# The softmax shift of a batch as one bias number of the exponential, with the start of the kernel listed anew

## The chip, the cores and the metric

The kernel runs on one core of a Trainium2 chip. The metric is the device time of one execution in microseconds (us); lower is better. TensorE (PE in the tables) multiplies matrices; VectorE (DVE) and ScalarE (ACT) work on tiles of 128 partitions; GpSimd (POOL) takes some elementwise work; SyncE (SP) issues most DMAs.

## The reference, cut to what matters

The input is 4 batches of 1024 tokens with 128 channels. Three layers run one after the other, each with its layer norm and its residual: a feed-forward layer with a router, attention with 16 heads of 8 channels, and the same feed-forward layer again.

```python
x = x + 0.5 * ffn(layernorm(x))        # relu(x @ up.T)**2 @ down.T + two of 8 experts
q, k, v = rotary(layernorm(x) @ qkv_w.T)
attn = einsum('bhqd,bhkd->bhqk', q, k) * SCALE
attn = attn + minimum(pos_k - pos_q, 0) * slopes[h] * 8.0
x = x + (softmax(attn) @ v) @ proj_w.T + proj_b
x = x + 0.5 * ffn(layernorm(x))
```

A softmax may subtract any number from a row's scores before the exponential, since it drops out in the division. The kernel subtracts an upper bound of the scores (a product of the largest norms of q and k), which keeps the exponential in range.

## The kernel before

The tokens are cut into 8 chunks of 512, two for each batch. A job "A" of a chunk is its first feed-forward layer, the second layer norm and q, k and v. A job "C" is the attention's projection and the second feed-forward layer. Attention runs in **quads**: for 4 heads (a group), one chunk of queries and one tile of 128 keys, `score(n)` multiplies keys and queries into the PSUM tile `f_scores` (128 x 2048), `weight(n)` is one exponential on ACT from `f_scores` to `weights`, and `weigh(n)` multiplies these with the values into `f_acc`. There are 256 quads. `f_scores` exists once: `score(n)` waits for the exponential of quad n - 1, and the exponential of quad n waits for `score(n)`. `weights` exists twice. On the diagonal DVE multiplies with a table `ediag` in between.

All engines walk through the same numbered **steps**. The table `PLAN`, together with `FILLS` and `DIAGONALS`, says for each job in which step each of its pieces is issued, on PE (hidden, spread, outs, qk, value, norms, turn, gate), and by fixed offsets on the other engines. Quad n stands in step `HEAD_STEPS + n`; what lies before is called the head here: it holds the A jobs of chunks 0 and 1, which batch 0's attention needs, and the beginning of chunk 2. Each engine works in the order of its list, so a piece that waits holds up all that stands behind it on that engine. In the head, the norm matmul's output and others use `f_acc` and `f_bank_o`; in the rest `f_bank_h` is shared by the pieces of the jobs.

The shift of a batch is made at the end of its second chunk: `norms` (PE) and `largest_norms` (DVE) for q and k, `bound_product` (DVE), `root` (POOL), `bound_minus` (DVE), which leaves -bound for each of 16 heads in `f_minus`. Before the change `fill_shift` (DVE) spreads it over 512 columns (`f_shift`), and `load_shift_rows` copies these rows by DMA into row 4 of each head's 32 rows of the query operand `q_op`; the key operands have 1.0 there, so that the score matmul itself subtracts the bound. `score` waits for these DMAs by `first_loaded` (batch 0) or `qk_loaded`. The other rows of `q_op`, `k_full` and `k_plain` are the parts of q and k, which are stored to DRAM (L780) and loaded again (L821 for batch 0, L2313 later), and rows of positions, which ACT writes (`fill_rows`, L1187).

The exponential of before, and the wait of its quad:

```python
def weight(n):
    act.wait_ge(scores_made, n + 1)
    if n >= 2:
        act.wait_ge(weighed, n - 1)
    nc.scalar.activation(weights[:, n % 2, :, :], scores[:, :, :], ACT.Exp).then_inc(exps_done, 1)
```

Of the kernel before, what the change touches and what calls it, by code (L numbers as in the profile page):

```python
# [21 lines left out]
F32 = mybir.dt.float32  # L22
F32R = mybir.dt.float32r
BF16 = mybir.dt.bfloat16
ALU = mybir.AluOpType
# [428 lines left out]
class Job:  # L454

    def __init__(self, index, kind, chunk, plan):
# [14 lines left out]
        if self.first:  # L471
            self.moments2, self.centre2, self.turn2 = plan["norm2"]
            self.qk, self.value, self.norms = plan["qk"], plan["value"], plan["norms"]
            at["product"] = [step + 1 for step in self.qk]
            at["sums"] = [at["product"][1], at["product"][3]]
            at["high"] = [step + 1 for step in at["sums"]]
            at["square_qk"] = at["high"]
            at["low"] = [step + 1 for step in at["high"]]
            at["largest"] = [step + 1 for step in self.norms]
            at.update(take_xt2=self.turn2 + 1, take_low2=self.turn2 + 1, take_v=self.value[1] + 1,  # L480
                      moments2=self.moments2 + 1, power2=self.moments2 + 1,
                      bound=at["largest"][1] + 1, minus=at["largest"][1] + 2, fill=at["largest"][1] + 2)
            if self.batch >= 1:
                at["fill"] = max(at["fill"], HEAD_STEPS + HALVES * HG * KT * (self.batch - 1) + 6)
# [10 lines left out]
HEAD_STEPS = 222  # L495
FILLS = (2, 69, 151, 118, 6, 109, 51, 59)
DIAGONALS = (136, 133, 156, 137, 141, 142, 144, 123, 132, 125, 146, 122, 139, 147, 131, 128)
PLAN = (
    ("A", 0, dict(front=(0, 0, 0), norm=(-9, -9, -9, 0), route=(8, 13, 18, 23, 28), coef=35, hidden=(3, 7, 12, 21, 25,
        30, 41, 49), spread=(39, 48, 55, 62), outs=(15, 15, 27, 27, 32, 32, 44, 44, 52, 52, 56, 56, 64, 64, 70, 70),  # L500
        residual=77, norm2=(80, 93, 124), qk=(140, 143, 150, 157), value=(152, 152), norms=(168, 183), own=dict(rectify=(10,
        14, 17, 26, 29, 36, 45, 54), square=(11, 20, 24, 31, 34, 42, 47, 58), scale=(46, 50, 57, 65), exp_logits=4,
        take_coef=38, moments2=85, power2=89, take_xt2=127, take_low2=134, take_v=161, product=(145, 153, 162, 166),
        sums=(155, 167), high=(160, 172), low=(164, 175), square_qk=(159, 171), largest=(173, 198), statistics=-9,
        moments=-9, power=-9, take_xt=-9, take_low=-9))),
    ("A", 1, dict(front=(0, 0, 0), norm=(1, 16, 19, 37), route=(43, 53, 60, 67, 72), coef=90, hidden=(61, 68, 73, 78,
        83, 91, 99, 107), spread=(98, 106, 114, 119), outs=(75, 75, 86, 86, 94, 94, 102, 102, 111, 111, 115, 115, 120, 120,
        126, 126), residual=130, norm2=(138, 158, 163), qk=(174, 176, 179, 182), value=(187, 187), norms=(191, 199),
        own=dict(rectify=(63, 71, 76, 84, 87, 96, 103, 112), square=(66, 74, 79, 88, 95, 100, 105, 116), scale=(101, 108,
        117, 121), exp_logits=40, take_coef=92, moments2=148, power2=154, take_xt2=165, take_low2=170, take_v=193,  # L510
        product=(177, 178, 184, 188), sums=(181, 190), high=(186, 196), low=(189, 200), square_qk=(185, 195), largest=(194,
        202), statistics=1, moments=5, power=9, take_xt=22, take_low=33, bound=205, minus=210, fill=212))),
    ("A", 2, dict(front=(0, 0, 0), norm=(97, 113, 129, 222), route=(223, 224, 225, 226, 227), coef=228, hidden=(203,
        208, 214, 221, 227, 230, 231, 232), spread=(230, 231, 232, 233), outs=(223, 223, 224, 224, 225, 225, 226, 226, 233,
        234, 234, 236, 236, 237, 237, 238), residual=239, norm2=(240, 242, 243), qk=(245, 247, 248, 249), value=(250, 251),
        norms=(252, 253), own=dict(xload=77, moments=104, power=110, take_xt=149, take_low=201, rectify=(206, 211, 216, 222,
        228, 231, 232, 233), square=(209, 215, 217, 222, 231, 232, 233, 234)))),
    ("A", 3, dict(front=(0, 0, 0), norm=(222, 227, 233, 235), route=(236, 237, 238, 243, 245), coef=246, hidden=(238,
        239, 240, 241, 242, 255, 256, 257), spread=(248, 255, 256, 257), outs=(245, 246, 247, 249, 250, 251, 252, 253, 254,
        254, 258, 259, 259, 261, 261, 262), residual=263, norm2=(264, 266, 267), qk=(269, 270, 271, 272), value=(273, 274),  # L520
        norms=(275, 276), own=dict(xload=130))),
    ("A", 4, dict(front=(0, 0, 0), norm=(243, 245, 258, 260), route=(261, 262, 263, 264, 265), coef=266, hidden=(262,
        263, 264, 265, 266, 268, 280, 281), spread=(268, 269, 281, 282), outs=(270, 271, 272, 273, 274, 275, 276, 278, 278,
        279, 279, 280, 285, 285, 286, 286), residual=287, norm2=(288, 290, 291), qk=(293, 296, 298, 299), value=(300, 301),
        norms=(303, 304))),
    ("A", 5, dict(front=(0, 0, 0), norm=(266, 268, 282, 284), route=(285, 286, 291, 293, 294), coef=295, hidden=(287,
        288, 289, 290, 292, 302, 307, 308), spread=(297, 303, 307, 308), outs=(293, 294, 294, 295, 296, 297, 297, 298, 300,
        301, 306, 306, 310, 310, 312, 312), residual=313, norm2=(314, 316, 317), qk=(320, 321, 322, 323), value=(324, 325),
        norms=(326, 327))),
    ("A", 6, dict(front=(0, 0, 0), norm=(291, 301, 309, 311), route=(312, 313, 315, 317, 318), coef=319, hidden=(313,  # L530
        314, 315, 316, 318, 329, 330, 331), spread=(321, 329, 330, 331), outs=(319, 320, 322, 323, 324, 325, 326, 327, 328,
        328, 332, 333, 333, 335, 335, 336), residual=337, norm2=(338, 340, 341), qk=(343, 345, 347, 348), value=(349, 350),
        norms=(351, 352))),
    ("C", 0, dict(front=(260, 269, 277), norm=(302, 310, 332, 334), route=(335, 336, 338, 341, 343), coef=344,
        hidden=(336, 337, 338, 339, 340, 353, 354, 355), spread=(346, 353, 354, 355), outs=(343, 344, 345, 346, 346, 347,
        348, 349, 350, 351, 356, 357, 357, 359, 360, 361), residual=362)),
    ("A", 7, dict(front=(0, 0, 0), norm=(316, 334, 356, 358), route=(359, 360, 361, 363, 364), coef=365, hidden=(359,
        360, 361, 362, 368, 369, 370, 371), spread=(369, 370, 371, 372), outs=(363, 363, 364, 364, 365, 366, 366, 368, 373,
        373, 375, 375, 376, 376, 377, 377), residual=378, norm2=(379, 381, 382), qk=(384, 385, 386, 387), value=(388, 389),
        norms=(390, 391))),  # L540
    ("C", 1, dict(front=(292, 302, 305), norm=(336, 357, 372, 374), route=(375, 376, 377, 379, 380), coef=381,
        hidden=(378, 379, 380, 383, 392, 393, 394, 398), spread=(392, 393, 394, 398), outs=(384, 385, 386, 387, 388, 389,
        390, 391, 395, 395, 396, 396, 397, 397, 402, 402), residual=403)),
    ("C", 2, dict(front=(363, 366, 367), norm=(369, 374, 399, 401), route=(402, 403, 404, 405, 406), coef=407,
        hidden=(403, 404, 409, 410, 413, 414, 415, 419), spread=(413, 414, 415, 419), outs=(405, 405, 406, 406, 411, 411,
        412, 412, 416, 416, 417, 417, 418, 418, 423, 423), residual=424)),
    ("C", 3, dict(front=(404, 407, 408), norm=(410, 412, 420, 422), route=(423, 424, 425, 426, 427), coef=428,
        hidden=(424, 425, 430, 431, 434, 435, 436, 440), spread=(434, 435, 436, 440), outs=(426, 426, 427, 427, 432, 432,
        433, 433, 437, 437, 438, 438, 439, 439, 444, 444), residual=445)),
    ("C", 4, dict(front=(425, 428, 429), norm=(432, 434, 441, 443), route=(444, 445, 446, 447, 448), coef=449,  # L550
        hidden=(445, 446, 451, 452, 455, 456, 457, 461), spread=(455, 456, 457, 461), outs=(447, 447, 448, 448, 453, 453,
        454, 454, 458, 458, 459, 459, 460, 460, 465, 465), residual=466)),
    ("C", 5, dict(front=(446, 449, 450), norm=(452, 454, 462, 464), route=(465, 466, 467, 468, 469), coef=470,
        hidden=(466, 467, 472, 473, 476, 477, 478, 479), spread=(476, 477, 478, 479), outs=(468, 468, 469, 469, 474, 474,
# [2084 lines left out]
```

## Time and profile before

| | |
|---|---|
| three runs | 807.15, 807.54, 807.88 us (median 807.54) |
| the profiled execution | 807.31 us, its span 805.5 us |
| PE busy | 742.4 us (92%) |
| ACT busy | 601.2 us (75%) |
| DVE busy | 445.9 us (55%) |
| POOL busy | 211.3 us (26%) |
| granted clock of PE, mean | 0.985 |

The span runs from the first to the last instruction of the profiled execution; 1.8 us of its time lie outside. The first exponential of a quad starts at 83.85 us and the last one at 744.62 us, so there are three stretches: the head, the quads with the jobs' pieces between them, and the rest of the last job. PE's weight loads (PEld) overlap its matmuls, and the ends of matmuls are modelled, so the busy share of PE says less than what it waits for.

### The profile page before, as it was taken

How to read it: one execution, taken by the hardware profiler on the slowest of the kernel's cores; microseconds unless marked ns; L12 is line 12 of the kernel's file. 1: busy time of each engine (PE TensorE's matmuls, PEld its weight loads, DVE VectorE, ACT ScalarE, POOL GpSimd, SP SyncE). 2: the span in 40 equal slices, each digit the busy share in tenths (PEclk: the TensorE clock that was granted, in tenths of full speed). 3: DMA queues.
4: the chain of work that ended last, by engine and by line, in shares of the span. 5: the costliest groups of instructions: out<-in, count | busy, mean ns of one | idle time of the engine just before them, and what ended most of it. 6: DMA issues, size and time to landing. Idle time of an engine off the chain costs nothing.

```text
span 805.5 us, 14520 instructions
## 1 busy us (share of the span) xinstructions
PE 742.4 (92%) x5520; PEld 370.6 (46%) x5520; DVE 445.9 (55%) x1155; ACT 601.2 (75%) x488; POOL 211.3 (26%) x184
## 2 busy tenths in 40 slices
PE   5996989999999999999999999999989999999876
PEld 3883534444444434344354443443434444434664
DVE  5776445826735773655654656445536435354664
ACT  3892578788878878978878888788878878888321
POOL 2125122223412341332332232321121311211443
PEclk9997799999999999999999999999999999999999
DMA  7015323122166120115332200144322002020200
GB/s 244 1 53 165 104 57 83 28 84 71 42 155 162 46 83 4 33 56 151 77 85 67 55 5 18 47 125 107 71 49 57 5 4 60 4 57 5 60 13 18
DMA packets 43966, 52.60 MB, mean 65 GB/s; under 512 B 10154, under 2 KB 28146, under 8 KB 43762
## 3 DMA queue, kind: packets, MB, share of 16 engines
q1 hardware_dynamic: 42066, 50.19, 23.6%
q10 hardware_dynamic: 1824, 1.41, 0.6%
q8 instruction: 46, 0.75, 0.4%
q14 instruction: 30, 0.25, 0.1%
HBM read 31.91 MB, written 19.40 MB: 64 GB/s over the span
## 4 chain that ended last, share of the span: by engine, by line
PE 67%; ACT 18%; DVE 7%; issue 3%; DMA 1%; POOL 0%; POOLq 0%; DVEq 0%; ACTq 0%
PE f_acc L927 22%; ACT weights L1232 17%; PE f_scores L908 14%; PE f_bank_o L1026 14%; PE f_bank_h L882 9%; PE f_bank_c L1005 1%; DVE weights L1572 1%; PE f_scores L882 1%; PE f_bank_h L951 1%; PE f_bank_c L970 1%; ACT f_relu L1160 1%; PE f_acc L1026 1%; PE f_bank_h L1058 1%; PE f_bank_c L972 1%; DVE f_xn L1327 1%
## 5 line engine op out<-in xcount | busy, mean ns | idle before, releaser
L1232 ACT ACTIVATE weights<-f_scores 128x2048 f32<-128x2048 f32 x256 | 480.8, 1878 | 119.7 <-PE f_scores L908 113.4
L927 PE MATMUL f_acc<-weights,v_res 128*9 128x512 f32 x2048 | 269.9, 596 | 8.8 <-DVE weights L1572 7.2
L1026 PEld LDWEIGHTS f_bank_o<-w_out,f_hid 128*128 128x128 f32 x960 | 121.9, 195 | 59.2 <-issue 50.7
L1026 PE MATMUL f_bank_o<-w_out,f_hid 128*128 128x128 f32 x960 | 146.8, 292 | 1.3 <-POOL f_hid L1270 1.0
L1572 DVE TENSOR_TENSOR weights<-weights,ediag 128x512 f32<-128x512 f32 x128 | 92.7, 724 | 97.8 <-ACT weights L1232 97.3
L1270 POOL TENSOR_TENSOR f_hid<-f_hid,f_relu 128x512 f32<-128x512 f32 x56 | 78.9, 1411 | 201.8 <-DVE f_hid L1462 199.4
L1270 POOL TENSOR_TENSOR f_hid<-f_relu 128x512 f32<-128x512 f32 x56 | 60.5, 1083 | 210.7 <-ACT f_relu L1160 210.6
L908 PE MATMUL f_scores<-q_op,k_plain 29*128 29x512 f32 (+3 forms) x768 | 86.6, 440 | 15.2 <-ACT weights L1232 10.3
L908 PEld LDWEIGHTS f_scores<-q_op,k_plain 29*128 29x128 f32 x768 | 37.4, 183 | 131.6 <-ACT weights L1232 110.6
L1160 ACT ACTIVATE f_relu<-f_bank_h 128x512 f32<-128x512 f32 x110 | 65.4, 595 | 31.2 <-PE f_bank_h L882 30.8
L882 PE MATMUL f_bank_h<-xn_t,w_hi 128*128 128x512 f32 x224 | 83.7, 455 | 5.1 <-ACT f_relu L1160 3.2
L1462 DVE TENSOR_TENSOR f_hid<-f_relu,f_bank_c 128x512 f32<-128x512 f32 x56 | 38.4, 685 | 86.3 <-ACT f_relu L1160 62.3
L908 PE MATMUL f_scores<-q_op,k_full 29*128 29x512 f32 (+3 forms) x640 | 62.2, 376 | 6.0 <-ACT weights L1232 5.0
L927 PEld LDWEIGHTS f_acc<-weights,v_res 128*9 128x9 f32 x2048 | 31.7, 88 | 68.3 <-issue 58.4
L882 PEld LDWEIGHTS f_bank_h<-xn_t,w_hi 128*128 128x128 f32 x224 | 35.0, 194 | 52.8 <-issue 27.3
L908 PEld LDWEIGHTS f_scores<-q_op,k_full 29*128 29x128 f32 x640 | 31.7, 186 | 49.1 <-ACT weights L1232 45.4
L882 PE MATMUL f_bank_h<-xn_t,w_lo 128*128 128x512 f32 x112 | 45.6, 407 | 0.0
L1258 POOL TENSOR_TENSOR rstd<-veps,minus_half 128x4 f32<-128x4 f32 x23 | 23.3, 1013 | 70.1 <-DVE veps L450 70.1
L1563 DVE COPY f_o_out<-f_acc 128x512 f32<-128x512 f32 x32 | 22.0, 688 | 30.2 <-PE f_acc L927 30.2
L1286 POOL TENSOR_TENSOR f_squares<-f_roped 128x512 bf16<-128x512 f32 x16 | 19.5, 1216 | 55.8 <-DVE f_roped L1506 42.7
L1005 PE MATMUL f_bank_c<-f_coef_t,spread_rows 128*128 128x512 f32 x58 | 24.0, 414 | 0.8 <-DVE f_hid L1462 0.8
L882 PEld LDWEIGHTS f_bank_h<-xn_t,w_lo 128*128 128x128 f32 x112 | 21.7, 194 | 5.4
(216 smaller groups left out, 716.1 us busy)
## 6 DMA issues: line engine op xcount, KB each, us to landing
q_parts<-f_parts SPq DMA_DIRECT2D x24, 256.0 KB, 3.0
k_parts<-f_parts SPq DMA_DIRECT2D x24, 256.0 KB, 3.0
q_op<-q_parts SPq DMA_DIRECT2D x48, 96.0 KB
k_full<-k_parts SPq DMA_DIRECT2D x48, 96.0 KB
k_plain<-k_parts SPq DMA_DIRECT2D x48, 96.0 KB
o_scratch<-f_o_out SPq DMA_DIRECT2D x128, 18.0 KB
x_ln<-in_L_attn_x_dram SPq DMA_DIRECT2D x8, 256.0 KB, 3.4
rope<-const_rope SPq DMA_DIRECT2D x1, 2048.0 KB, 10.7
```

What stands on the lines that cost most here:

```text
L882: last = nc.tensor.matmul(out, w[:, col:col + P], x_t[:, part, :], start=(i == 0), stop=(i == 2))
L908: last = nc.tensor.matmul(scores[:, j, lo:hi], k_op[rows, g, kt * P:(kt + 1) * P], q_op[rows, g, CHUNK * half + lo:CHUNK * half + hi], sta ...
L927: last = nc.tensor.matmul(acc[BLOCK * j:BLOCK * j + VW, :], v_res[:, c // HALVES, kt, col:col + VW], weights[:, n % 2, j, :], start=(kt == ...
L1005: nc.tensor.matmul(spread_bank(job, m), spread_rows[:, m * P:(m + 1) * P], coef_t[:, :], start=True, stop=True).then_inc(spread, 1)
L1026: last = nc.tensor.matmul(out_bank(job)[:, t * P:(t + 1) * P], hid[:, m, t * P:(t + 1) * P], w_out[:, m, :], start=(m == 0 and t == 0), st ...
L1160: nc.scalar.activation(relu_tile(job, m), hidden_bank(job, m), ACT.Relu).then_inc(relu_ready, 1)
L1232: nc.scalar.activation(weights[:, n % 2, :, :], scores[:, :, :], ACT.Exp).then_inc(exps_done, 1)
L1258: nc.gpsimd.tensor_tensor(rstd[:, which, :], veps[:, which, :], minus_half[:, :], ALU.pow).then_inc(rstd_ready[which], 1)
L1270: nc.gpsimd.tensor_tensor(hid[:, m, :], other, relu_tile(job, m), ALU.mult).then_inc(hid_ready, 1)
L1462: v.tensor_tensor(hid[:, ST + m, :], relu_tile(job, ST + m), spread_bank(job, m), ALU.mult).then_inc(scaled_ready, 1)
L1563: v.tensor_copy(o_out[:, :], acc[:, :]).then_inc(acc_read, 1)
L1572: v.tensor_tensor(at, at, ediag[:, GH * g:GH * (g + 1), :], ALU.mult).then_inc(diag_done, 1)
```

## The change

The shift of a batch becomes one number: the smallest of the 16 heads' -bound, so the largest bound, for all heads. It is given to the exponential as its bias, from the tile `minus_all` (128 partitions x 4 batches). To put the number on all 128 partitions, a matmul (`cast_bounds`, PE) multiplies `f_minus`, broadcast over 128 columns, with the identity: its output holds all 16 values on each partition, and a DVE reduction takes the smallest. The rows `f_shift`, their 32 DMAs and the waits for them are gone; row 4 of `q_op` stays zero, as `fill_rows` writes it. The first exponential of each batch waits for the reduction (`shift_ready`).

```diff
+            def cast_bounds(job):
+                b = job.batch
+                if not job.head:
+                    bank_h_read("cast", job, 0)
+                else:
+                    pe.wait_ge(norms_read, 2 * HEAD_JOBS)
+                pe.wait_ge(bound_step, 4 * b + 3)
+                nc.tensor.matmul(side_bank(job)[:, 0:HEADS], minus[:, b:b + 1].broadcast_to([HEADS, P]),
+                                 ident[0:HEADS, 0:HEADS], start=True, stop=True).then_inc(bounds_cast, 1)
...
             def fill_shift(job):
-                b = job.batch
-                dve.wait_ge(bound_step, 4 * b + 4)
-                for g in range(HG):
...
-                v.tensor_scalar(shift[:, :], rope[0:HEADS, 0, 0:CHUNK], 0.0, minus[:, b:b + 1], ALU.mult,
-                                ALU.add).then_inc(shift_ready, 1)
+                dve.wait_ge(bounds_cast, job.batch + 1)
+                v.tensor_reduce(minus_all[:, job.batch:job.batch + 1], side_bank(job)[:, 0:HEADS], AX.X,
+                                ALU.min).then_inc(shift_ready, 1)
...
-                nc.scalar.activation(weights[:, n % 2, :, :], scores[:, :, :], ACT.Exp).then_inc(exps_done, 1)
+                batch, first = divmod(n, HALVES * HG * KT)
+                if first == 0:
+                    act.wait_ge(shift_ready, batch + 1)
+                nc.scalar.activation(weights[:, n % 2, :, :], scores[:, :, :], ACT.Exp,
+                                     bias=minus_all[:, batch:batch + 1]).then_inc(exps_done, 1)
...
-                    pe.wait_ge(first_loaded[g], 16 * (PART_LOADS + HALVES))
+                    pe.wait_ge(first_loaded[g], 16 * PART_LOADS)
...
-                if step == FIRST_JOB[1].at["fill"] + 1:
-                    sp.wait_ge(shift_ready, 1)
+                if step == FIRST_JOB[1].at["store"][1] + 1:
                     load_half(1, 0, late_plain, late_loaded)
                     load_half(0, 1, first_loaded[1], first_loaded[1])
-                    load_shift_rows(sp, 0, 1, first_loaded[1])
...
-HEAD_STEPS = 222
-FILLS = (2, 69, 151, 118, 6, 109, 51, 59)
+HEAD_STEPS = 223
+FILLS = (78, 58, 177, 118, 125, 134, 128, 122)
```

`PLAN` is a new table as a whole. Counted from the first quad, most pieces of the A jobs of chunks 2 to 6 stand one to a few steps earlier and some of chunk 4's later; those of the C jobs from chunk 3's on stand, but for a few by one step, where they stood. Two places of the new order are shown, as the program's lists have them; the line numbers of the changed kernel are some 8 to 10 off.

PE from chunk 1's q and k to the first quad. `f_xn_t` with `w_hi` and `w_lo` as weights at L882 are the four q and k matmul groups, at L1058 (L1050 after) the values, L1071 (L1063) the norms; `f_bank_h<-xn_t` are hidden tiles of chunk 2, L970 and L972 (L962 and L964) its gate, L908 (L898) `score`. Before, the stretch from the end of the values:

```order
L1058 MATMUL f_scores<-w_lo,f_xn_t 128x128
L1071 MATMUL f_acc<-f_squares,headsum 16x512 x2
L882 MATMUL f_bank_h<-xn_t,w_hi 128x512 x2
L882 MATMUL f_bank_h<-xn_t,w_lo 128x512
L882 MATMUL f_bank_h<-xn_t,w_hi 128x512 x2
...
L908 MATMUL f_scores<-q_op,k_plain 128x128 x4
L908 MATMUL f_scores<-q_op,k_full 128x384 x4
L970 MATMUL f_bank_c<-w_gate,xn_t 128x16
L972 MATMUL f_bank_c<-w_gate,xn_t 128x8
```

The same stretch of the changed kernel, from the last group of chunk 1's k:

```order
L872 MATMUL f_scores<-f_xn_t,w_lo 128x512
L962 MATMUL f_bank_c<-w_gate,xn_t 128x16
...
L1063 MATMUL f_acc<-f_squares,headsum 16x512
L872 MATMUL f_bank_h<-xn_t,w_hi 128x512 x2
L872 MATMUL f_bank_h<-xn_t,w_lo 128x512
L1063 MATMUL f_acc<-f_squares,headsum 16x512
L872 MATMUL f_bank_h<-xn_t,w_hi 128x512 x2
L872 MATMUL f_bank_h<-xn_t,w_lo 128x512
L1074 MATMUL f_acc<-ident,f_minus 128x16
L898 MATMUL f_scores<-q_op,k_plain 128x128 x4
L898 MATMUL f_scores<-q_op,k_full 128x384 x4
L1018 MATMUL f_bank_o<-w_out,f_hid 128x128 x4
```

Before, four hidden tiles stand between the norms and the first score, and the gate behind it. After, the gate and three hidden tiles stand ahead, with the two norm matmuls between the tiles; the values (not in these rows) moved from behind the q and k groups to behind the first of them.

ACT from the transposed second norm of chunk 0 (`f_xn_t<-f_bank_o`) on; `f_parts<-f_roped` is the high part of q or k, `ediag` a table of a head, `q_op` and `k_full` are filled with rows of positions. Before:

```order
L1136 ACTIVATE f_xn_t<-f_bank_o 128x512
L1191 ACTIVATE ediag<-weights,slope 128x128 x12
L1136 ACTIVATE xn_t<-f_bank_h 128x512
L1187 ACTIVATE q_op<-weights,q_add,row_sel 128x1024
L1191 ACTIVATE ediag<-weights,slope 128x128
L1136 ACTIVATE f_parts<-f_roped 128x512
```

and after:

```order
L1141 ACTIVATE f_xn_t<-f_bank_o 128x512
L1192 ACTIVATE q_op<-weights,q_add,row_sel 128x1024
L1192 ACTIVATE k_full<-weights,k_add,row_sel 128x1024 x4
L1196 ACTIVATE ediag<-weights,slope 128x128 x4
L1141 ACTIVATE f_parts<-f_roped 128x512
L1141 ACTIVATE v_res<-f_scores 128x64x8
L1196 ACTIVATE ediag<-weights,slope 128x128 x7
```

Five fills of 1024 columns moved to here from the feed-forward part of the head, and stand ahead of chunk 0's high part of q.

## Rows read from the trace of the kernel before

**Rows 1.** Page: the chain that ended last, by engine.

```profile
PE 67%; ACT 18%; DVE 7%; issue 3%; DMA 1%; POOL 0%; POOLq 0%; DVEq 0%; ACTq 0%
```

**Rows 2.** The chain in order of time: start us, us, what, up to the first quad.

```profile
77.81 4.95 DMA q_op<-f_shift
82.89 0.93 PE f_scores L908 x7
```

**Rows 3.** Timeline of the head's end: start us, us, engine, line, operation [idle before].

```profile
70.14 1.48 DVE L1513 TENSOR_TENSOR f_roped<-f_turn_a,f_turn_b 128x512 f32<-128x512 f32 x1
75.03 0.14 DVE L1544 TENSOR_SCALAR f_minus<-f_bound 16x1 f32<-16x1 f32 x1 [0.65 <-POOL f_bound L1292]
77.12 1.92 SPq L780 DMA_DIRECT2D k_parts<-f_parts  x3
83.49 1.52 SPq L821 DMA_DIRECT2D k_plain<-k_parts  x4
```

**Rows 4.** Windows: busy time by engine, granted clock of PE, DMA share, GB/s.

```profile
76.00:80.00 4.00, 2.74 (x6) 1.16 (x4) 0.52 (x3) 1.13 (x2) 1.68 (x2) 0.50 0.84 261
84.00:88.00 4.00, 3.82 (x23) 3.51 (x24) 2.07 (x12) 3.23 (x3) 0.00 (x0) 0.50 0.48 114
```

**Rows 5.** Exponentials: the group, then the first and the last of 256 in the timeline.

```profile
L1232 ACT ACTIVATE weights<-f_scores 128x2048 f32<-128x2048 f32 x256 | 480.8, 1878 | 119.7 <-PE f_scores L908 113.4
83.85 1.88 ACT L1232 ACTIVATE weights<-f_scores 128x2048 f32<-128x2048 f32 x1 [1.45 <-PE f_scores L908]
744.62 1.88 ACT L1232 ACTIVATE weights<-f_scores 128x2048 f32<-128x2048 f32 x1 [0.17 <-PE f_scores L908]
```

**Rows 6.** Timeline of ACT in one quad, from exponential to exponential.

```profile
98.78 1.88 ACT L1232 ACTIVATE weights<-f_scores 128x2048 f32<-128x2048 f32 x1 [0.64 <-PE f_scores L908]
100.64 0.60 ACT L1160 ACTIVATE f_relu<-f_bank_h 128x512 f32<-128x512 f32 x1
101.27 1.88 ACT L1232 ACTIVATE weights<-f_scores 128x2048 f32<-128x2048 f32 x1
```

**Rows 7.** Groups on ACT by shape: busy us, mean ns of one.

```profile
L309 ACT ACTIVATE proj_t<-prep 128x128 f32<-128x128 f32 x1 | 0.3, 277 | 1.0 <-PE prep L356 1.0
L1136 ACT ACTIVATE xn_t<-f_bank_h 128x512 fp32r<-128x512 f32 x14 | 8.3, 594 | 6.2 <-PE f_bank_h L960 6.2
L1136 ACT ACTIVATE f_parts<-f_roped 128x512 fp32r<-128x512 f32 x4 | 2.5, 631 | 5.3 <-DVE f_roped L1506 4.4 <-DVE f_roped L1513 0.8
L1191 ACT ACTIVATE ediag<-weights,slope 128x128 f32<-128x128 f32 x16 | 5.0, 387 | 0.0
L1187 ACT ACTIVATE k_full<-weights,k_add,row_sel 128x1024 fp32r<-128x1024 f32 x4 | 4.9, 1227 | 0.0
```

**Rows 8.** Timeline of the head from chunk 1's last outputs to chunk 0's loads.

```profile
52.81 1.06 PE L1026 MATMUL f_acc<-w_out,f_hid 128*128 128x128 f32 x8
...
55.25 0.73 PE L882 MATMUL f_bank_o<-f_xn_t,w_hi 128*128 128x512 f32 x2 [0.94 <-DVE f_xn_t L1485]
...
63.71 0.63 ACT L1136 ACTIVATE f_parts<-f_roped 128x512 fp32r<-128x512 f32 x1 [0.61 <-DVE f_roped L1513]
...
66.06 1.81 SPq L780 DMA_DIRECT2D k_parts<-f_parts  x3
...
70.39 1.56 SPq L821 DMA_DIRECT2D k_plain<-k_parts  x4
```

**Rows 9.** Window of the values' line alone (chunk 1): busy PE, PEld.

```profile
69.00:71.00 2.00, 1.55 (x12) 1.41 (x12) 1.00 0.40 138
```

**Rows 10.** The chain in order of time, within the quads.

```profile
614.94 0.51 PE f_scores L908 x4
615.45 1.09 PE f_bank_o L1026 x8
616.54 0.98 PE f_acc L927 x8
```

**Rows 11.** Timeline of POOL: the last batch's root.

```profile
531.04 0.54 POOL L1292 TENSOR_TENSOR f_bound<-f_product,f_half_power 16x1 f32<-16x1 f32 x1 [9.49 <-DVE f_product L1538]
```

More of the change, by code:

```diff
@@ L494 @@
 HEAD_JOBS = 2
[L495 to L497 removed]
+HEAD_STEPS = 223
+FILLS = (78, 58, 177, 118, 125, 134, 128, 122)
+DIAGONALS = (169, 155, 183, 142, 160, 138, 140, 158, 172, 137, 150, 151, 159, 2, 3, 153)
 PLAN = (
[L499 to L504, printed above, removed]
[L505 to L561 removed]
@@ new lines @@
+    ("A", 0, dict(front=(0, 0, 0), norm=(-9, -9, -9, 0), route=(6, 9, 17, 22, 29), coef=36, hidden=(4, 7, 11, 16, 23,
+        26, 41, 49), spread=(39, 48, 55, 61), outs=(13, 13, 20, 20, 32, 32, 44, 44, 51, 51, 56, 56, 63, 63, 68, 68),
+        residual=72, norm2=(80, 94, 114), qk=(126, 129, 133, 136), value=(139, 139), norms=(157, 170), own=dict(rectify=(8,
+        12, 19, 21, 28, 34, 46, 53), square=(10, 15, 24, 25, 31, 43, 47, 54), scale=(42, 50, 57, 64), exp_logits=5,
+        take_coef=37, moments2=85, power2=89, take_xt2=117, take_low2=123, take_v=147, product=(130, 132, 148, 152),
+        sums=(141, 161), high=(145, 167), low=(154, 171), square_qk=(144, 166), largest=(165, 174), statistics=-9,
+        moments=-9, power=-9, take_xt=-9, take_low=-9))),
@@ new lines @@
+    ("A", 1, dict(front=(0, 0, 0), norm=(1, 27, 30, 38), route=(45, 52, 59, 66, 74), coef=81, hidden=(60, 67, 71, 79,
+        83, 91, 97, 106), spread=(96, 104, 113, 119), outs=(73, 73, 86, 86, 93, 93, 100, 100, 109, 109, 116, 116, 120, 120,
+        124, 124), residual=127, norm2=(135, 156, 162), qk=(173, 181, 185, 187), value=(176, 176), norms=(198, 208),
+        own=dict(rectify=(62, 69, 75, 87, 92, 98, 103, 110), square=(65, 70, 82, 90, 95, 101, 108, 112), scale=(99, 107,
+        115, 121), exp_logits=40, take_coef=84, moments2=143, power2=149, take_xt2=164, take_low2=168, take_v=182,
+        product=(178, 184, 190, 193), sums=(186, 197), high=(192, 203), low=(196, 207), square_qk=(191, 202), largest=(200,
+        210), statistics=1, moments=14, power=18, take_xt=33, take_low=35, bound=212, minus=215, cast=216, fill=217))),
@@ new lines @@
+    ("A", 2, dict(front=(0, 0, 0), norm=(88, 111, 146, 189), route=(205, 223, 224, 225, 226), coef=227, hidden=(194,
+        201, 209, 226, 227, 229, 230, 231), spread=(229, 230, 231, 232), outs=(223, 223, 224, 224, 225, 225, 228, 228, 232,
+        233, 233, 235, 235, 236, 236, 237), residual=238, norm2=(239, 241, 243), qk=(245, 246, 247, 248), value=(249, 250),
+        norms=(251, 252), own=dict(xload=72, rectify=(199, 206, 211, 227, 228, 230, 231, 232), square=(223, 223, 223, 227,
+        230, 231, 232, 233), scale=(230, 231, 232, 233), moments=102, power=105, take_xt=175, take_low=180, exp_logits=195,
+        take_coef=228))),
@@ L562 @@
+    ("C", 7, dict(front=(486, 489, 490), norm=(492, 494, 495, 497), route=(498, 499, 500, 501, 502), coef=503,
+        hidden=(497, 497, 498, 498, 499, 505, 505, 506), spread=(505, 505, 506, 506), outs=(499, 499, 499, 499, 500, 500,
+        500, 500, 508, 508, 508, 508, 509, 509, 509, 509), residual=510)),
 )
@@ L569, with largest_through @@
 STEPS = JOBS[-1].residual + 1
+def largest_through(job, side):
+    return sum(at <= job.at["largest"][side] for other in JOBS[0:HEAD_JOBS] for at in other.at["largest"])
 def uses_of_bank_h():
@@ L1112, in tokens @@
                                 norms(job, side)
+                        if job.half == 1 and job.at["cast"] == step:
+                            cast_bounds(job)
             pe.wait_ge(env["w_ready"], 2)
```

85 lines of the change are left out of this document (51 added, 34 removed).

## The prediction

> **What bounds the kernel now.** I read the page first. The chain that ended last is PE's in two thirds and ACT's in under a fifth [rows 1], so the question is what holds PE. The timeline gives three stretches. The head lasts until the first exponential at 83.85; the quads take 744.62 - 83.85 = 660.8 us for 255 intervals, 2.59 each [rows 5]; the tail follows.
>
> In the quads the reader should see a loop of two engines. With one `f_scores`, an exponential (1.88), the score behind it, and the next exponential run strictly one after the other: in the quad shown 101.27 - 98.78 = 2.49 us [rows 6]. That is the floor of an interval. The starts of all 256 exponentials (the first and last stand in [rows 5]) give this picture: 141 of the 255 intervals are below 2.525, 40 lie between 2.525 and 2.585, and 74 above, where PE's own pieces (score, a job's pieces, `weigh`) fill more than the loop leaves. A quad of the second kind is score 0.51, two outs 1.09 and `weigh` 0.98 [rows 10]: 2.58. So PE is nearly full and yet more than half of the intervals are set by the loop through ACT. ACT's busy share of 75% hides this: its idle 119.7 us before exponentials is almost all a wait for the score [rows 5], that is, the other half of the loop.
>
> The head's end has another limit. The chain runs through the DMA of the shift rows, 4.95 us, to the first score at 82.89 [rows 2]. -bound was there at 75.03 [rows 3]; its rows then shared the DMA engines with the stores of chunk 1's k, issued at 77.12, at a DMA share of 0.84 [rows 3, 4].
>
> **The exponential's bias.** This is the part that the diff makes look free. Before, the exponential has numbers for scale and bias; after, it reads a bias of one value per partition. What does such an operand cost? The groups on ACT have operations of both kinds [rows 7]. A plain copy of 128x128 from PSUM takes 277 ns. Of 512 columns, PSUM takes 594 and SBUF 631, so SBUF costs 37 more. `ediag`, 128x128 from SBUF with one such operand, takes 387: 387 - 277 - 37 = 73 ns. A fill has two of them on 1024 columns of SBUF: a copy would take 631 plus 512 more columns at (594 - 277)/384 = 0.826 ns, 1054; the fill takes 1227, so 173 for two, 87 each [rows 7]. I take 85 ns, as the fills are longer and so nearer to the exponential. The bounds: 73 below, and 110 above (`ediag` against the PSUM copy, if the SBUF share were nothing).
>
> The operand is read by every exponential, so it lengthens the loop's floor from 2.49 to 2.575. It doesn't lengthen intervals that PE fills beyond that. Replacing each of the 255 intervals by the larger of itself and 2.575 adds 12.6 us; with 73 ns it is 10.5, with 110 ns 17.1. If the operand's read hides behind a preceding ACT operation, as where a relu runs directly ahead of an exponential [rows 6], less is added: of 256 exponentials 179 waited for a score, so about 12.6 x 179/256 = 8.8. I take 12.6 and keep 8.8 and 17.1 for the range.
>
> The Trainium skill speaks against the change here too (*ScalarE: Activation LUTs*, "What ACT_TABLE_LOAD costs"): an ACTIVATE with numbers as scale and bias takes 186 ns + 0.833 ns a column, and each per-partition pointer operand adds about 93 ns. The trace agrees for the first kind: 1892 by the page at 2048 columns, 1878 in the row [rows 5]. With 93 ns the same replacement of intervals would add 14.0 us.
>
> **The head.** Without the shift's DMA the first score needs chunk 0's loads and its place on PE, and the first exponential needs the reduction as well.
>
> Until PE has finished the feed-forward work (chunk 1's last outputs end near 53.9 [rows 8]), it is busy without a gap and has the same pieces in both lists. The fills taken out of there free ACT, which PE didn't wait for: nothing. Then chunk 0's low part of the second norm comes before, not behind, chunk 1's residual on DVE, and q's first group can start at 53.9 instead of 55.25 [rows 8]. Against this ACT has five fills (5 x 1.23 [rows 7]) and four tables ahead of q's high part. I follow the lists: k's high part then comes at about 63.4 instead of 63.71, and its low part on POOL is not behind a square, so the store is issued near 65.4 instead of 66.06 [rows 8]. Chunk 0's loads, 12 DMAs issued from 70.39 on [rows 8], go 0.7 earlier.
>
> Chunk 1's groups start behind chunk 0's in both lists, but its values, 12 matmuls in 1.55 us [rows 9], now stand between its groups, and chunk 2's gate (8 matmuls of at most 16 columns, estimated 0.9 us) ahead of its norms. I follow its chain: k's sum ends near 72.7 instead of 71.62 [rows 3], -bound is there near 76.3 instead of 75.03 [rows 3]. Chunk 2's third hidden tile runs until then on PE. The cast, one small matmul, and the reduction behind it I estimate at 0.3 us each with their semaphores; the score, issued beside the reduction, takes 0.95 (82.89 to 83.85 [rows 2, 5]). The first exponential so starts at about 78.0, if the clock is 2.4 GHz in these matmuls; at 1.2 GHz, as before at 76 to 80 [rows 4], near 79.8. I take 78.0 for 83.85: -5.8. The bounds are -4 and -8; the latter if the clock stays up and the first ten quads, which took 29.0 us instead of 24.9 partly at 1.2 GHz [rows 4], lose less too.
>
> The work that is left at that moment is the same. Before, four hidden tiles of chunk 2 were done and its gate was not; after, three and the gate, each about 0.9 us.
>
> **The new list.** I priced each piece of a job in a quad's step with its time on PE (two outs 1.09 [rows 10]; by the chain's pieces hidden, qk and gate 0.9, spread 0.24, and so on) and added over all quads what exceeds the loop's room: 2.49 less score and `weigh`, about 1.04 us. Before this is 22.7 us, after 22.0. The old table's sum agrees with the 660.8 - 255 x 2.49 = 25.9 us that the intervals really have above the floor. So the new table is worth -0.7; as the prices are rough, -2.5 to +1.5. The three casts in the quads add 3 x 0.1 on PE, at most 0.3 us together, if PE is the limit there.
>
> **The other edits.** 30 of SP's issues of 0.5 us and three fills of `f_shift` on DVE vanish; no quad waited for either, so nothing. The cast waits on PE, in order, for POOL's root: score and `weigh` of the next quads stand behind it. The root stands two steps ahead, about 5 us, takes 0.54 and finds POOL idle, before the last for 9.49 us [rows 11], so I cost it at nothing. The loads of `late_plain` follow the stores of chunk 1's k: k_plain's issues at 83.49 ran 6.4 us behind those stores [rows 3], and now start near 82.8, land near 86.5, and quad 4 wants them at 88 or later.
>
> **Sum.** 807.3 (the profiled execution; 0.2 below the median of the runs) - 5.8 (head) + 12.6 (bias operand) - 0.7 (list) + 0.2 (casts) = 813.6 us.
>
> **Rivals.**
> 1. *The operand costs nothing on the path* (ACT reads it while it waits for the score, as it is idle before 179 exponentials). Then 813.6 - 12.6 = 801.0, faster. For it: the idle time is there [rows 5]. Against: `ediag` and the fills show the operand inside the instruction's own time, and a semaphore wait stands ahead of an instruction's work, not beside it. This is the case on the other side. It decides from 0.047 us per exponential: there the loop's loss equals the head's gain. 13%.
> 2. *The head gains little*, since the moved values and the fills on ACT delay chunk 1's k, or the late loads are waited for. With -2 in place of -5.8: 817.4. The rows leave some 2 us of room in each of these places, so 12%.
> 3. *The gain and the loss nearly cancel*: read hidden behind preceding operations (+8.8) and the clock up at the first quads (-8) and a list at -1.5: 806.8. 10%.
> 4. *A cast stalls PE* in each of the three batches, behind POOL, 2 us each: 819.6. Only POOL work right ahead of a root could do it, and the row shows none [rows 11]. 5%.
>
> **Numbers.** My forecast, slower through the bias operand, has 60%, its own range 810 to 817. With 0.2% (1.6 us), about what a measurement of this kernel can tell: faster 0.17 (rival 1 and a part of 3), same 0.09, slower 0.74. The range is 807.0 to 818.5: it takes in the 8.8 and 17.1 of the operand and rival 2, and leaves out rival 1 and the far end of rival 4.
>
> **What would show it.** The exponential's row: 1963 ns instead of 1878, with the shortest intervals at 2.575; if it reads 1878, the operand's cost is wrong. The first exponential near 78.0, and no DMA in the chain there; DVE's reduction directly ahead of it. The last exponential near 83.85 + 660.8 - 5.8 + 12.1 = 751. If the row is longer and the intervals are not, rival 1 holds. If the first exponential is later than 80, look at chunk 1's k sum and at the clock from 74 on.

## The result: slower, and by more than forecast

The changed kernel takes 826.27 us (median of 4 runs, 823.51 to 829.06) against 807.66 before: a ratio of 1.0238, 95% interval 1.0215 to 1.0262. Forecast were 813.6 and at most 818.5. Its profiled execution took 828.2, its span 826.4. Its runs lie 5.5 us apart; those of before that stand beside them lie 0.7 apart. The kernel before, run 17 to 23 times beside each group of experiments, spread over 7 to 8 us around medians of 807.2 to 807.3. Two runs far off the others, 1165.7 of `r6_filler_quads` (mean granted clock 0.56) and 842.48 of `r12_fillers_no_operand` (0.85), are left out of the times below.

The page of after. The first row is its busy time; the second answers to the group in [rows 5].

```profile
PE 753.7 (91%) x5528; PEld 373.9 (45%) x5528; DVE 442.2 (54%) x1155; ACT 621.3 (75%) x488; POOL 209.5 (25%) x184
...
L1240 ACT ACTIVATE weights<-f_scores,f_minus_all 128x2048 f32<-128x2048 f32 x256 | 503.9, 1969 | 127.4 <-PE f_scores L898 118.6
```

An exponential with the operand takes 1969 ns instead of 1878. From the starts in the timeline, 160 of the 255 intervals of after are 2.57 to 2.62: that is the new floor, 2.58. The first exponential starts at 80.86 (before 83.85), the last at 766.26 (before 744.62). So the head gave 3.0 back and the quads took 685.4 instead of 660.8, 24.6 more.

Two more views show what the quads lost. The first is the waits of PE (us in total, times, longest), the row of before and that of after.

```profile
PE f_scores L908 <- ACT weights L1232: 15.3, 32, 1.1
```

```profile
PE f_scores L898 <- ACT weights L1240: 25.8, 72, 1.2
```

The second is the windows of after (columns as in [rows 4]): one of full clock and those of the first fall of the clock behind the first ten quads.

```profile
244.00:248.00 4.00, 3.55 (x36) 1.91 (x28) 1.22 (x2) 3.39 (x2) 0.00 (x0) 1.00 0.18 41
248.00:250.00 2.00, 1.89 (x17) 1.37 (x14) 1.52 (x5) 1.39 (x3) 0.00 (x0) 0.66 0.00 0
250.00:252.00 2.00, 2.00 (x13) 0.86 (x12) 0.93 (x3) 1.04 (x1) 0.00 (x0) 0.50 0.00 0
```

And the timeline of after in that place, quads 61 to 63:

```profile
245.82 0.39 PE L898 MATMUL f_scores<-q_op,k_plain 29*128 29x256 f32 x4 [0.45 <-ACT weights L1240]
...
246.26 0.28 PE L962 MATMUL f_bank_c<-w_gate,xn_t 128*128 128x16 f32 x1
...
248.96 2.07 PE L1018 MATMUL f_bank_o<-w_out,f_hid 128*128 128x128 f32 x8
249.07 1.97 ACT L1240 ACTIVATE weights<-f_scores,f_minus_all 128x2048 f32<-128x2048 f32 x1 [0.61 <-PE f_scores L898]
...
253.01 1.97 ACT L1240 ACTIVATE weights<-f_scores,f_minus_all 128x2048 f32<-128x2048 f32 x1 [1.97 <-PE f_scores L898]
```

PE idled for 0.45 us behind an exponential, ran the gate's small matmuls, and then its granted clock fell to 0.50, which is 1.2 GHz. Two outs, 1.09 in [rows 10], took 2.07, and the interval of quad 62 became 3.94. The windows show four such stretches in the quads of after, at quads 62, 119, 201 and 222, and none in the quads of before. This and what is said of falls below leaves aside the first ten quads, in which the clock was at 0.50 in both profiles (84 to 90 before, 82 to 88 after). The forecast had no term for falls.

### The profile page after: what moved, and what is told of

Same layout as the page of the kernel before. It is cut to its first block and busy times, and to the rows that moved or that the text cites. A ratio compares the mean times of both kernels' runs of the same rounds, so it can differ in the third digit from the quotient of the medians.

```text
span 826.4 us, 14500 instructions
## 1 busy us (share of the span) xinstructions
PE 753.7 (91%) x5528; PEld 373.9 (45%) x5528; DVE 442.2 (54%) x1155; ACT 621.3 (75%) x488; POOL 209.5 (25%) x184
## 5 line engine op out<-in xcount | busy, mean ns | idle before, releaser
L1240 ACT ACTIVATE weights<-f_scores,f_minus_all 128x2048 f32<-128x2048 f32 x256 | 503.9, 1969 | 127.4 <-PE f_scores L898 118.6
L1018 PEld LDWEIGHTS f_bank_o<-w_out,f_hid 128*128 128x128 f32 x960 | 123.6, 197 | 62.7 <-issue 53.9
L1018 PE MATMUL f_bank_o<-w_out,f_hid 128*128 128x128 f32 x960 | 149.3, 296 | 1.9 <-POOL f_hid L1276 1.6
L1276 POOL TENSOR_TENSOR f_hid<-f_hid,f_relu 128x512 f32<-128x512 f32 x56 | 77.0, 1377 | 179.3 <-DVE f_hid L1468 175.5
L898 PE MATMUL f_scores<-q_op,k_plain 29*128 29x512 f32 (+3 forms) x768 | 87.2, 442 | 21.5 <-ACT weights L1240 18.1
L898 PEld LDWEIGHTS f_scores<-q_op,k_plain 29*128 29x128 f32 x768 | 37.7, 183 | 143.7 <-ACT weights L1240 122.5
L898 PE MATMUL f_scores<-q_op,k_full 29*128 29x512 f32 (+3 forms) x640 | 62.4, 376 | 8.1 <-ACT weights L1240 7.7
L898 PEld LDWEIGHTS f_scores<-q_op,k_full 29*128 29x128 f32 x640 | 32.1, 187 | 53.0 <-ACT weights L1240 48.5
L1292 POOL TENSOR_TENSOR f_squares<-f_roped 128x512 bf16<-128x512 f32 x16 | 18.6, 1161 | 70.2 <-DVE f_roped L1512 57.9
```

Source lines behind the costliest of these rows:

```text
L898: last = nc.tensor.matmul(scores[:, j, lo:hi], k_op[rows, g, kt * P:(kt + 1) * P], q_op[rows, g, CHUNK * half + lo:CHUNK * half + hi], sta ...
L1018: last = nc.tensor.matmul(out_bank(job)[:, t * P:(t + 1) * P], hid[:, m, t * P:(t + 1) * P], w_out[:, m, :], start=(m == 0 and t == 0), st ...
L1276: nc.gpsimd.tensor_tensor(hid[:, m, :], other, relu_tile(job, m), ALU.mult).then_inc(hid_ready, 1)
```

## The experiments

**The theory** after the result: the operand lengthens the loop as priced, and the longer wait gives PE idle time in which its clock falls (A). The rival: the new list, with light steps around the gates, makes the clock fall whatever the exponential takes (B). The first four kernels cross the two.

`r1_no_operand`, the changed kernel with one edit:

```diff
-                nc.scalar.activation(weights[:, n % 2, :, :], scores[:, :, :], ACT.Exp,
-                                     bias=minus_all[:, batch:batch + 1]).then_inc(exps_done, 1)
+                nc.scalar.activation(weights[:, n % 2, :, :], scores[:, :, :], ACT.Exp).then_inc(exps_done, 1)
```

> The changed kernel with its exponential's bias taken away: the cast, the reduction and the wait for it stay, the shift is left out of the scores. Theory A (the operand lengthens the loop of score and exponential, and the idle time that this gives PE lets its clock fall within the quads): the exponential takes 1878 ns, the floor of an interval is 2.49, the four stretches at 1.2 GHz within the quads are gone, and the time is 826.3 - 13.5 (floor) - 8 (clock) = about 805. Theory B (the new list, with light steps behind the gates, lets the clock fall, whatever the exponential takes): 826.3 - 13.5 = about 813, with stretches at 0.5 near the same quads (62, 119, 201, 222).

Measured: 809.72 (12 runs, 804.0 to 813.28), 1.0021 (0.9995 to 1.0048). So about 16.6 of the 18.6 us are the operand's. The median lies between A's 805 and B's 813, and the windows show one fall of the clock in the quads, at quad 201: in this list the clock can fall without the operand. A is mostly right, B has a part. The head of this kernel is that of after, and yet in this profile its first exponential starts at 82.55 and not at 80.86: its clock was at 0.50 from 64 to 86, that of after at 1.00 from 72 to 80. A single profile doesn't give the head closer than that.

`r2_operand_added`, the kernel before with one edit (`zero_all` is set once, ahead):

```diff
-                nc.scalar.activation(weights[:, n % 2, :, :], scores[:, :, :], ACT.Exp).then_inc(exps_done, 1)
+                nc.scalar.activation(weights[:, n % 2, :, :], scores[:, :, :], ACT.Exp,
+                                     bias=zero_all[:, batch:batch + 1]).then_inc(exps_done, 1)
```

> The kernel before with one edit: its exponential reads a bias of one zero per partition. List, head and shift rows stay. Theory A: the exponential takes 1965 ns, 807.5 + 13 = 820.5 from the floor, and more, up to 829, if the clock falls in the quads here too. Theory B: 820.5 with a full clock in all quads. If the operand cost nothing on the path: 807.5.

Measured: 826.89 (822.1 to 828.44), 1.0228 (1.0196 to 1.026). One operand of zeros alone costs all that the change costs, 19.6 us. The clock fell twice in the quads of its profile, at 250 and 564. B's 820.5 is out.

`r3_old_list`, the changed kernel with the table of before, the cast's step set to 221:

> The changed kernel (cast, reduction, bias operand, no shift rows) with the table of steps, fills and diagonals of before; the first cast stands directly ahead of the first score. Theory A: as the changed kernel, 822 to 828, since the operand is there. Theory B: 807.5 + 13 from the floor - what the head gains without the shift's DMA (3 to 6) = 815 to 818, and no stretch at 0.5 in the quads.

Measured: 830.85 (827.9 to 833.77), 1.0291 (1.026 to 1.0323), outside both ranges. The first exponential came at 83.05 only, since I had put the cast behind the four hidden tiles of chunk 2:

```profile
74.76 0.14 DVE L1549 TENSOR_SCALAR f_minus<-f_bound 16x1 f32<-16x1 f32 x1 [0.65 <-POOL f_bound L1297]
...
82.31 0.17 DVE L1555 TENSOR_REDUCE f_minus_all<-f_acc 128x1 f32<-128x16 f32 x1 [7.35 <-PE f_acc L1073]
```

-bound lay ready for 7 us. Of the four falls in its quads, those at 252, 566 and 624 say the same as r2's: the old list doesn't protect from them once the operand is there. The one at 378 has a cause of its own. There the cast of batch 2 held PE up, and the interval of quad 109 became 5.34 (2.92 in before):

```profile
378.91 0.39 PE L1073 MATMUL f_bank_h<-ident,f_minus 16*128 16x16 f32 x2 [1.36 <-ACT f_relu L1164]
```

`r4_old_shift`, the kernel before with the new table alone:

> The kernel before with the new table alone (shift rows by DMA, no bias operand). Theory A: the quads take 661 as before, give or take 2, the clock stays up in them, and the first exponential comes near 84: 806 to 810. Theory B: the clock falls in the quads, 813 to 817.

Measured: 811.91 (12 runs, 810.37 to 819.62), 1.0069 (1.0045 to 1.0094). In the profile the quads took 660.2 without a fall, against 660.8 before; behind the first ten intervals 632.5 against 631.8. The loss is in the head: -bound came at 81.67, the shift rows' DMA behind it, and the first exponential at 88.5. So the head of the new list doesn't suit the old shift. Four of the 12 runs took 815 to 820, for which no profile is there.

`r5_both_operands`, r2 with a scale of ones beside the bias of zeros:

> The kernel before with two operands on its exponential, a bias of zeros and a scale of ones, one value per partition each. Theory A (each operand lengthens the instruction, and with it every interval that the loop of score and exponential sets): the exponential takes 1878 + 2 x 91 = 2060 ns, the floor is 2.67, and the replacement of intervals by the larger of themselves and 2.67 adds some 32 us in all, so 840, and a few us for stretches at 1.2 GHz, to 848. Rival (a second operand rides with the first): as with one operand, 827.

Measured: 848.77 (846.87 to 850.06), 1.0505 (1.0476 to 1.0534). The exponential's row, and ahead of it that of r2:

```profile
L1236 ACT ACTIVATE weights<-f_scores,f_zero_all 128x2048 f32<-128x2048 f32 x256 | 503.8, 1968 | 121.3 <-PE f_scores L909 112.5
```

```profile
L1236 ACT ACTIVATE weights<-f_scores,f_zero_all,f_one_all 128x2048 f32<-128x2048 f32 x256 | 527.0, 2059 | 120.9 <-PE f_scores L909 111.4
```

90 and 91 ns for each operand, and the floor rises with it: 2.49, 2.58, 2.67. The replacement of before's intervals by 2.67 gives 30.7; the measured 41.6 leave 10.9. In the profile the quads with a fall (62, 63, 194, 200, 201, 243) hold 9.1 above the replacement, the other quads 3.8.

**Does the idle time make the clock fall?** `r6_filler_quads` fills it in the changed kernel:

```diff
+            def fill(n, step):
...
+                for i in range(max(int((1.1 - load_of(step)) / 0.25), 0)):
+                    j = i % GH
+                    nc.tensor.matmul(acc[BLOCK * j:BLOCK * j + VW, :], zero_w[:, :],
+                                     ediag[:, 0:GH, :].rearrange("p h t -> p (h t)"), start=False, stop=False)
```

> The changed kernel with filler matmuls on TensorE in the 35 quads whose steps hold little else: 1 to 4 matmuls of 9x512 with a weight of zeros, added into the accumulator behind the quad's weigh, where the engine would idle. The quads ahead of the four falls of the clock (59, 117, 198, 219) are among them. Theory A (the clock falls because the engine idles just before): no stretch at 1.2 GHz in the quads, so 826.3 - 8 = 818, less 0.5 for fillers that are too long; runs within 2 us of each other. Rival (the falls don't hang on that idle time): stretches at 1.2 GHz at the same places, 826 to 828.

Measured: 834.15 (5 runs, 833.42 to 835.23), 1.0329 (1.0307 to 1.0352). The windows show full clock in all quads behind the first few, and the runs lie within 2 us as A says, but the time is far from its 818: the fillers were too many. Many of the quads that got them grew by 0.3 to 0.85, and all quads together took 11.7 us more than in r7. The result supports A, but slower quads may themselves have helped, which `r10_few_fillers` tries. The remedy as sized is worse than the fall.

`r7_route_later`, the changed kernel with one number changed, for the head:

```diff
-    ("A", 2, dict(front=(0, 0, 0), norm=(88, 111, 146, 189), route=(205, 223, 224, 225, 226), coef=227, hidden=(194,
+    ("A", 2, dict(front=(0, 0, 0), norm=(88, 111, 146, 189), route=(218, 223, 224, 225, 226), coef=227, hidden=(194,
```

> The changed kernel with one number of its table changed: the first router step of chunk 2 on VectorE stands at 218 instead of 205, behind the reductions of chunk 1's norms instead of ahead of the last of them. Theory A (that step, whose operations took 1.2 us and more, made the last norm's reduction late, 78.05 for a matmul that ended at 76.77): the last norm_max starts near 77.0, -bound is there near 78.7, and the first exponential starts 1.0 to 1.3 earlier than 80.86, if the clock is as there; 825.2. Rival (the wait of those operations was for something else on the same path): no change.

Measured: 825.31 (820.94 to 829.0), 1.0224 (1.0193 to 1.0255). The head of after, by its timeline, and then that of r7:

```profile
76.33 1.19 DVE L1379 TENSOR_SCALAR f_sfc<-f_en 128x32 f32<-128x32 f32 x1
...
78.05 0.67 DVE L1535 TENSOR_REDUCE norm_max<-f_acc 16x1 f32<-16x512 f32 x1
```

```profile
77.03 0.68 DVE L1535 TENSOR_REDUCE norm_max<-f_acc 16x1 f32<-16x512 f32 x1 [0.97 <-PE f_acc L1063]
```

The last norm's reduction comes 1.0 earlier, -bound at 78.73 instead of 79.74, and so does the first exponential, at 79.85. In the totals this doesn't show: the runs still lie 8 us apart. Its profiled execution had one fall (quad 201) and quads of 679.2. At quad 62, where after lost its clock, PE idled as long here, ahead of the same matmuls, and kept its clock:

```profile
244.05 0.39 PE L898 MATMUL f_scores<-q_op,k_plain 29*128 29x256 f32 x4 [0.46 <-ACT weights L1240]
```

So this idle time alone doesn't decide whether the clock falls. The runs' times go with their mean granted clocks: 820.9 to 824.9 at 0.983 to 0.991, 825.7 to 829.0 at 0.971 to 0.979.

`r8_filler_head` puts 30 fillers into the head of the kernel **before**, each a 128x512 matmul into a bank that nothing uses then:

```diff
+            def fill(count):
+                for _ in range(count):
+                    nc.tensor.matmul(bank_c[:, :], w_hi[:, 0:P], w_hi[:, 0:CHUNK], start=True, stop=True)
+
             def turn2(job):
+                if job.twin:
+                    pe.wait_ge(scaled_ready, RT * HEAD_JOBS)
+                    fill(7)
```

> The kernel before with 30 filler matmuls of 128x512 (into the bank of the coefficients, which nothing uses then) in the head's gaps of TensorE from 59.6 to 82.9. Theory A (idle time lets the clock fall): the clock stays at 2.4 GHz from 62 to 92, where it was at 1.2 for 21 us; the first exponential stays near 83, since the shift's DMA sets it, and the first ten quads take 25 to 26 instead of 29.0: 807.5 - 3.5 = 804. Rival (the clock falls there by some other cause): 1.2 GHz as before, and 807.5 or up to 2 more for fillers that last longer at 1.2.

Measured: 802.7 (12 runs, 800.51 to 807.28), 0.9954 (0.9936 to 0.9972). The clock stays at 1.00 from 24 until 81.5. Here too the quicker runs had the higher mean clock: 800.5 to 804.7 in the nine at 0.991 to 0.999, 804.5 at 0.986, 806.9 and 807.3 at 0.982. And the first exponential came at 78.56, not near 83: -bound was there at 72.74 instead of 75.03, its DMAs were issued at 74.19, ahead of chunk 1's stores and not among them, and the four hidden tiles ran at full clock.

`r9_filler_head2` adds four fillers behind chunk 2's gate:

> The kernel before with the 30 fillers of r8_filler_head and four more behind chunk 2's gate, ahead of the second score, where the engine idled for 0.99 us in r8 before its clock fell at 81.9. Theory A: no stretch at 1.2 GHz near 82 to 85, the interval of 3.88 there gets near 2.6, the first ten quads take 26.5 instead of 28.2: 802.7 - 1.5 = 801. Rival: no change, 802.7.

Measured: 800.35 (798.95 to 802.34), 0.9915 (0.9889 to 0.994). The first ten quads take 26.6 instead of 28.2. This is the fastest kernel here: the one before, with its old shift, and 34 matmuls that compute nothing. Its clock was at 0.50 from 18 to 24, as in several other profiles, and nothing shows a cost of that: the feed-forward part ended at 52.6, and at 53.9 in before, which had 1.00 there. Windows of its head; those of before show 0.80, 0.63 and 0.50 for the same stretches:

```profile
64.00:72.00 8.00, 7.92 (x38) 5.26 (x37) 7.48 (x11) 1.87 (x3) 5.38 (x5) 1.00 0.38 119
72.00:80.00 8.00, 7.33 (x39) 4.88 (x38) 2.37 (x9) 3.66 (x5) 4.71 (x5) 1.00 0.57 161
80.00:88.00 8.00, 8.00 (x71) 4.27 (x70) 5.18 (x23) 6.25 (x5) 1.01 (x1) 1.00 0.53 154
```

**The change with its clock held up.** `r10_few_fillers` is r7 with few fillers in the quads (`3 if load_of(step) == 0 else 1 if load_of(step) <= 0.6 else 0`), none on the diagonal:

> The changed kernel with the router step of r7_route_later moved and few fillers in the quads: 3 matmuls of 9x512 where a step holds nothing else, 1 where it holds a transpose or half an out, none on the diagonal, so that they fit in the idle time. Theory A: the falls at quads 62, 119, 201 and 222 are gone or fewer, the quads take 676 to 678: 825.3 - 3 to - 6 = 819 to 822. Rival (fillers in r6 only seemed to work, by making every quad longer): as r7_route_later, 825.

Measured: 824.52 (821.64 to 826.43), 1.0208 (1.0178 to 1.0238). The profile has one fall in the quads, at quad 119, whose light step ahead (117) lies on the diagonal and so got no filler, and the head runs at 1.2 GHz from 64 to 72 and again from 80. From r7 it can't be told, in time or in the number of falls. A's 819 to 822 is missed, and its rival's 825 met.

`r11_fillers_all` adds fillers in the head:

```diff
             def turn2(job):
+                if job.twin:
+                    keep(6)
...
+                if job.head and (side == 1 or not job.twin):
+                    keep(2 if job.twin else 4 if side else 5)
...
+                if job.head:
+                    keep(5)
```

> r10_few_fillers with 22 fillers of 128x512 in the head's gaps (ahead of the norms of chunk 0, the second transpose of chunk 1, the last norm and the cast), into a bank of the scores that nothing uses then. Theory A (the head's gain was smaller than forecast because its matmuls ran at 1.2 GHz and a router step stood ahead of the last norm): the clock stays up from 63 to 80, the first exponential starts near 77.0, which is below the 78.56 that the old mechanism reaches with such fillers, and the time is 4 below r10: 816. Rival (something else sets the head's end): the first exponential stays near 79.5.

Measured: 818.71 (817.76 to 819.87), 1.0137 (1.0111 to 1.0162). The clock is 1.00 from 26 through the rest of the head and all quads, the first exponential starts at 76.95, and the runs lie 2.1 us apart. A's 816 is missed by 2.7. Its time is 5.8 below r10: 2.3 from the head's end, 1.8 from the first quads and 1.6 from quad 119. The list and the fillers of the quads are those of r10, so that quad 119 kept its clock here isn't the doing of a filler in the quads.

`r12_fillers_no_operand` takes the bias away from it, as in r1:

> r11_fillers_all without the bias of the exponential, so with no shift subtracted: its distance to r11 is the operand's price with the clock held up. By the replacement of the intervals it is 13.5; if the operand costs more than the floor by other ways than the clock, more, up to the 17 to 20 of the pairs without fillers. By theory A: 816 - 13.5 = 802.5.

Measured: 804.7 (11 runs, 803.36 to 807.49), 0.9969 (0.9948 to 0.999). Its distance to r11 is 14.0, and 13.6 between the two profiled executions.

## Why the prediction was wrong

**The operand: right in mechanism, size and place.** 85 ns were forecast, 91 measured. The Trainium skill (*ScalarE: Activation LUTs*, "What ACT_TABLE_LOAD costs") states about 93 for each, and r5 agrees for the second one too, 91. With the clock held up, the operand costs 14.0 (r11 against r12); forecast were 12.6 from the replacement of intervals, and 13.5 follow with the measured floor of 2.58. It didn't hide behind preceding operations, and rival 1, which held that ACT reads it while it waits, is out: 160 intervals rose with it.

**What failed is the step "It doesn't lengthen intervals that PE fills beyond that", and with it the sum over intervals at a fixed clock.** The sum took PE's durations as given. But the wait that the operand adds on ACT is idle time on PE (25.8 us in 72 waits for 15.3 in 32; 15.0 in 33 in r1), and PE's clock fell behind such places. The profiled execution, 14.6 above the forecast, divides as follows:

| | forecast | measured |
|---|---|---|
| head | -5.8 | -3.0 |
| first ten intervals and floor | +12.6 | +13.9 |
| falls of the clock, 4 in the quads | 0 | +6.9 |
| intervals above the floor that hold the exponential as well | 0 | +2.4 |
| list | -0.7 | +0.6 |
| casts | +0.2 | +0.8 |
| tail | 0 | -0.7 |

The floor's 13.9 is 13.5 by replacement and 0.4 more in the first ten intervals. The falls are the excess of quads 61, 62, 119, 201, 202 and 222 over r7's intervals (5.5), and that of r7's own quads 200 and 201 over r4's, these raised to 2.58 (1.4). The 2.4 is what then remains; most of it is 0.05 to 0.11 in each of some thirty intervals that are longer than the floor and hold the exponential all the same, such as the last of a group: at quad 127 the score still waits for the exponential, and the interval is 2.71 for 2.63 in r4. That r2 costs 19.6 and r1 only 16.6, for 14.0 with the clock held up, I take to be falls as well: their number differs by list and by run, and it is not one I could have read from the profile of before.

How far the falls are shown to come with PE's idle time differs by place. At the head's end it is shown: the clock was at 0.50 there in before and at 1.00 in r8 and r9, whose gaps were filled. In the quads it is supported, not shown: filled kernels had no fall or one in their profiles (r6, r11, r12 none, r10 one), and the runs of r6 and r11 lie 1.8 and 2.1 us apart; but r7 had only one fall without any fillers, and quad 62 kept its clock with the idle time that it had in after, and r10 had one at quad 119 where r11, with the same quads, had none. Why quad 62 and not another light one is open, and so is why one run of a kernel has more falls than the next. Nor does every slow run show in the mean clock: before took 806.9 at 0.975 and 812.0 at 0.978.

**The head: the step "I follow its chain: k's sum ends near 72.7" failed.** k's sum ended at 75.13, and the first exponential came 2.9 behind the forecast 78.0. Three things made this up. "Until PE has finished the feed-forward work", the lists were to cost the same, but chunk 1's last outputs ended at 54.72 and not near 53.9, and q's first group started at 54.48, 0.6 behind the forecast. In the six profiles with the old list these outputs end between 52.4 and 54.6, in the eight with the new one between 54.0 and 55.2. Then I had followed PE's order for chunk 1 but not DVE's: four router operations stood ahead of the last norm's reduction, worth 1.0 (r7). The rest was the clock, 1.2 GHz for chunk 1's first groups and values (mean 0.57 from 64 to 72); with it held up, and the router step moved, k's sum ended at 71.68 and the first exponential came at 76.95 (r11), a little before my 78.0. But then the old shift reaches 78.56 (r8). So of the 4.95 us of DMA in [rows 2], which I had taken as the price of the old shift, the new one saves about 1.6 at full clock, by two kernels whose lists differ: in before the rows of the shift were late because PE was slow ahead of them and they fell among chunk 1's stores; r8 doesn't tell these two apart.

**The casts: rival 4 in small, and behind another engine.** The one of batch 2 held up a score, though POOL's root was long done:

```profile
372.19 0.59 ACT L1165 ACTIVATE f_relu<-f_bank_h 128x512 f32<-128x512 f32 x1
372.83 0.28 PE L1074 MATMUL f_bank_h<-ident,f_minus 16*128 16x16 f32 x1 [0.47 <-ACT f_relu L1165]
```

It waited for the relu that frees `f_bank_h`, which ACT does behind an exponential: that interval is 3.35 (3.34 in r1, r7 and r11), 2.58 in r4, which has no cast. In r3 the same wait was 1.36, and the clock fell right behind it.

**The list** was forecast as worth -0.7 and is worth +0.7 behind the first ten intervals (r4), or +0.6 with all intervals raised to the new floor. Its largest single loss is quad 81, 1.42: `weigh` waits there for a product on DVE that stands behind other work and takes 1.47 beside a multiplication of GpSimd's, which my prices of PE's pieces didn't see.

**The range** ended at 818.5, because I had summed bounds of terms that I knew, and none was for falls of the clock in the quads. Even with the clock held up and the router step moved the change takes 818.7, 5.1 above the forecast.

## What to carry to other kernels

An operand on the instruction that every interval of a loop contains costs the number of intervals at the floor times its own length, however idle the engine looks; read the distribution of intervals, not the busy share. Where TensorE waits in such a loop, its clock can fall in some executions and not in others, so compare the granted clock window by window over more than one profile and the mean clock of every run, and allow a term for it when a forecast adds waits. Idle gaps ahead of a serial stretch may be worth filling with matmuls that compute nothing, each counted against the gap: 34 of them gained 0.85% here, while fillers that overran their gaps lost more than the falls that they removed.

## What was unexpected in the hardware

Some of VectorE's operations take far longer beside GpSimd's: behind -bound in after, an addition of 128x24 took 2.24 us beside three of GpSimd's multiplications and ended with the last of them, and it took 0.17 us at 252.28, when GpSimd was idle. In r4 `f_shift` took 3.01 us instead of 0.47 beside three such multiplications, right in the chain to the first score.

```profile
79.68 3.02 POOL L1276 TENSOR_TENSOR f_hid<-f_relu 128x512 f32<-128x512 f32 x3
...
80.51 2.24 DVE L1393 TENSOR_TENSOR f_pair_sum<-f_sfc 128x24 f32<-128x24 f32 x1
...
252.28 0.17 DVE L1393 TENSOR_TENSOR f_pair_sum<-f_sfc 128x24 f32<-128x24 f32 x1
```

That the clock's falls differ between executions of one kernel was new to me as well: after and r7 have the same quads and had four falls and one in their profiles, and after and r1 have the same head and reached the first exponential at 80.86 and 82.55. No long idle time stood ahead of the first fall in after: none of PE's waits from 241 to 249 is longer than 0.45 us. The kernels with fillers mostly spread less, 1.8 to 4.1 us in r6, r9, r11 and r12, though 4.8 in r10 and 6.8 in r8, for 8 in r7 and in before.
